# Causal attention: five full half steps on the diagonal, shift rows passed on by GpSimd, maxima matmuls run once

## The chip, the cores and the metric

The kernel runs on one core of one Trainium2 chip. The metric is the device time of one execution in microseconds (us), compared by the median of several runs. The engines are named as in the profile: PE (TensorE matmuls) and PEld (its weight loads), DVE (VectorE), ACT (ScalarE), POOL (GpSimd) and SP (SyncE, which issues the DMAs).

## The reference, cut to what matters

Two transformer layers over 2048 tokens of width 128, with 16 heads of 8. The first has causal attention with rotary positions and a gated feed-forward network; the second has a low-rank attention without a mask and a mixture of eight experts. For the change only the attentions matter:

```python
# first attention
scores = jnp.einsum('bhsd,bhtd->bhst', q, k) / scale
scores = jnp.where(causal[None, None], scores, -jnp.inf)
attn = jax.nn.softmax(scores.astype(jnp.float32), axis=-1).astype(x.dtype)
out = jnp.einsum('bhst,bhtd->bhsd', attn, v)
# second attention: the same without the mask
attn = jnp.einsum('bhqd,bhkd->bhqk', query, key) / scale
attn = jax.nn.softmax(attn, axis=-1)
out = jnp.einsum('bhqk,bhkd->bhqd', attn, value)
```

## The kernel before

The program is a row of phases: norm, projection, attention, output projection, norm, feed-forward, norm, projection, second attention, output projection, norm, gate, experts. Each phase gives every engine its own instruction list, tied together by semaphores. The change is in `attention_phase` alone, which is called for both layers, and in the constant `EXTRA_PASSES`.

**Units.** An attention has 16 units (c, g): a block c of 512 queries (four) and a group g of four heads (four). Unit n needs the maximum over the keys for each of its queries. So the work of a unit is in two parts, made for different units at the same time. *Maxima*: `score_maxima` (PE, L424) computes scores with queries on partitions into a pair of banks, and DVE reduces them (`reduce`, L560). *Steps*: `scores` (L443) computes scores with keys on partitions, ACT takes the exponential (L540) into `k.probs`, and `values` (L456) multiplies with V and sums up in bank 7. The shift by the maxima is folded into extra rows of Q: DVE writes them to `shiftM` (L583, L587), PE turns them (`turn_shift`, L409), and ACT copies them into the rows 32 to 63 and 96 to 127 of Q, for both blocks of heads at once (`take_shift`, L525, two instructions of 32x1024).

**Steps and halves.** A step is one block of 128 keys, for four heads; it has two half steps b of two heads each. In the causal attention a unit has 4(c+1) steps. The last four lie on the diagonal, and `first_col` makes them 512, 384, 256 and 128 columns wide. POOL sets the triangle to zero there (`affine_select`, L509). In the second attention each unit has 16 steps, all full.

**The order on PE** is written out by hand in `unit(n)`: for each half step two score matmuls, then (in the half step where they are due) the queries of unit n+2 (L399, L401) or the turned shift of unit n+1, then the maxima that `plan(n)` gives to this half step, and then a part of the values of the step before. `plan` spreads the last reductions of unit n+1 and the first ones of unit n+2 over the half steps of unit n, in proportion to their widths; the former are urgent, because the shift of unit n+1 needs them. `shift_after` puts the shift two steps before the unit's end.

**Banks.** Scores, queries and the turned shift share three banks in turn (`wait_bank`), so a score matmul waits until ACT is done with what stood in its bank three jobs earlier. Maxima use two pairs of banks in turn: pair m waits for reduction m-2.

**Repetitions.** `score_maxima(m, i, passes)` repeats its pair of matmuls, with the same output, `passes` times: 3 in units with c=0, 2 with c=1, 1 with c=2 and 3 (first attention) and 1 in the units of the second. In the prologue, ahead of unit 0, it is 3 in both attentions.

Of the kernel before, what the change touches and what calls it, by code (L numbers as in the profile page):

```python
# [15 lines left out]
P = 128  # L16
# [5 lines left out]
CW = 512  # L22
# [12 lines left out]
EXTRA_PASSES = (2, 1, 0, 0)  # L35
# [271 lines left out]
def attention_phase(nc, k, layer):  # L307
# [5 lines left out]
    steps = [TC * (c + 1) if causal else T for c, g in units]  # L313
# [9 lines left out]
    first_col = lambda n, kt: max(0, kt - TC * units[n][0]) * P if causal else 0  # L323
# [4 lines left out]
    s_base = [sum(steps[:n]) for n in range(NU + 1)]  # L328

    shift_after = [steps[n] - 2 for n in range(NU)]  # L330

    def exp_bank_jobs():
        for n in (0, 1):
            yield from (("queries", n, b) for b in (0, 1))
        yield ("shift", 0)
        for n in range(NU):
            for kt in range(steps[n]):
                yield from (("scores", n, kt, j) for j in range(HG))
                if kt == 0 and n + 2 < NU:
                    yield from (("queries", n + 2, b) for b in (0, 1))  # L340
                if kt == shift_after[n] and n + 1 < NU:
                    yield ("shift", n + 1)

    e_number = {job: number for number, job in enumerate(exp_bank_jobs())}
    exp_job = lambda n, kt, j: e_number["scores", n, kt, j]

    masks = {n: TC * units[n][0] for n in range(NU)} if causal else {}
    mask_base = lambda n, kt: 2 * (TC * n + kt - masks[n])

    def plan(n):  # L350
        todo = last_reductions(n + 1) + first_reductions(n + 2)
        urgent = len(last_reductions(n + 1))
        widths = [CW - first_col(n, kt) for kt in range(steps[n]) for _ in (0, 1)]
        costs = [len(reductions(m)[i][1]) * (reductions(m)[i][3] + P) for m, i in todo]
        slots, done = [], 0
        for slot in range(len(widths)):
            enough = 0
            while enough < len(todo) and sum(costs[:enough]) * sum(widths) < sum(widths[:slot + 1]) * sum(costs):
# [3 lines left out]
            if slot >= 2 * shift_after[n]:  # L362
                enough = max(enough, urgent)
            if slot == len(widths) - 1:
# [7 lines left out]
    with ExitStack() as ctx:  # L372
        sem = lambda s: ctx.enter_context(nc.semaphore(f"{name}_{s}"))
        e_ready, e_done, pv_done, acc_free = sem("e_ready"), sem("e_done"), sem("pv_done"), sem("acc_free")
        m_ready, m_done, masked = sem("m_ready"), sem("m_done"), sem("masked")
        neg_ready, hi_ready, shift_ready, acc_zero = sem("neg_ready"), sem("hi_ready"), sem("shift_ready"), sem("acc_zero")
# [3 lines left out]
        acc = k.bank[7]  # L380

# [6 lines left out]
        def _(pe):  # L388
# [46 lines left out]
            def scores(n, kt, j):  # L435
                c, g = units[n]
                b, half = divmod(j, 2)
                rows = slice(HALF * half, HALF * half + HALF)
# [713 lines left out]
```

## Time and profile before

| | us |
|---|---|
| median of 3 runs | 1871.16 (1868.39 to 1871.88) |
| the profiled execution | 1862.05 |
| its span, first to last instruction | 1860.1 |

| engine | busy us | share of the span |
|---|---|---|
| PE | 1721.7 | 93% |
| PEld | 812.7 | 44% |
| DVE | 1159.5 | 62% |
| ACT | 1155.4 | 62% |
| POOL | 82.4 | 4% |

All rows of the trace come from the profiled execution, so a sum is made against its 1862.05 us. A line of the profile names the source line, the engine, the operation and the tiles, output first, and its shapes. In a timeline the first two numbers are start and length in us; what stands in brackets is the time for which the engine was idle before it, and what ended that. The granted clock is TensorE's: 1.00 is 2.4 GHz and 0.50 is 1.2 GHz. Matmuls are pipelined, so the distance between the starts of two groups says more of PE's pace than their lengths.

In the trace the first attention has its prologue from 56.5 to 74.0 us, the units with c=0 up to 144.3, c=1 up to 254.9, c=2 up to 396.3 and c=3 up to 561.8 (units 12 and 13 up to 484.8). The prologue of the second attention begins at 825.4 with its first maxima, and its units run from 881.5 to 1566.9.

### The profile page before, as it was taken

To read this page: it belongs to the slowest core of one execution; us is meant where nothing else is said; L and a number is where in the kernel's file an instruction comes from. 1 tells how busy PE (TensorE), PEld (TensorE's weight loads), DVE (VectorE), ACT (ScalarE), POOL (GpSimd) and SP (SyncE) were. 2 spreads that over 40 slices of the span, in tenths; PEclk is the share of its full clock that TensorE was granted. 3 is DMA by queue.
4 is the path that set the end of the run, shared out by engine and by line. 5 is a ranking of instruction groups with operands and counts; after the bars stand their busy time and mean duration, and the time that the engine had idled before them with its cause. 6 is when DMAs were issued, how large, how long until landed. Compare 5 with 4: busy or idle time off the path is not lost. (4 is left out here: it accounts for less than half of the span.)

```text
span 1860.1 us, 32237 instructions
## 1 busy us (share of the span) xinstructions
PE 1721.7 (93%) x13312; PEld 812.7 (44%) x13312; DVE 1159.5 (62%) x1566; ACT 1155.4 (62%) x2092; POOL 82.4 (4%) x158
## 2 busy tenths in 40 slices
PE   6899999999998999678999999999999999599999
PEld 3555444333335444334333333333333334467777
DVE  6576787888505111469899999999999852411111
ACT  3447678678883222231888888888888886143443
POOL 3011101000010000110000000000000000000000
PEclk9799999899998999779999999999999999699999
DMA  3100000000000000100000000000000000000000
GB/s 101 64 1 2 1 2 1 1 1 2 1 1 1 0 0 0 53 1 1 1 1 1 2 1 1 2 1 1 1 2 1 1 1 1 10 26 23 11 23 23
DMA packets 16769, 17.15 MB, mean 9 GB/s; under 512 B 2995, under 2 KB 13696, under 8 KB 16128
## 3 DMA queue, kind: packets, MB, share of 16 engines
q1 hardware_dynamic: 16639, 15.32, 2.6%
q8 instruction: 95, 1.56, 0.3%
q14 instruction: 35, 0.28, 0.1%
HBM read 14.26 MB, written 1.05 MB: 8 GB/s over the span
## 5 line engine op out<-in xcount | busy, mean ns | idle before, releaser
L560 DVE TENSOR_REDUCE maxp<-banks 128x2 f32<-128x1024 f32 (+3 forms) x800 | 945.0, 1201 | 194.1 <-PE banks L424 99.3
L540 ACT ACTIVATE probs<-banks 128x512 f32<-128x512 f32 (+3 forms) x1664 | 854.6, 571 | 222.8 <-PE banks L443 202.9
L456 PE MATMUL banks<-probs,V 128*9 128x256 f32 (+3 forms) x6272 | 491.3, 385 | 6.2 <-POOL probs L509 5.7
L443 PE MATMUL banks<-Q,K 64*128 64x512 f32 (+3 forms) x1664 | 449.8, 487 | 28.0 <-ACT Q L525 20.2
L424 PE MATMUL banks<-K,Q 64*128 64x512 f32 (+3 forms) x2232 | 421.7, 406 | 19.1 <-DVE maxp L560 17.5
L443 PEld LDWEIGHTS banks<-Q,K 64*128 64x128 f32 x1664 | 183.7, 186 | 394.6 <-ACT probs L540 306.8
L424 PEld LDWEIGHTS banks<-K,Q 64*128 64x128 f32 x2232 | 218.7, 194 | 71.9 <-DVE maxp L560 52.9
L456 PEld LDWEIGHTS banks<-probs,V 128*9 128x9 f32 x6272 | 93.2, 88 | 253.3 <-ACT probs L540 187.7
L952 DVE SCALAR_TENSOR_TENSOR x<-banks,wts,x 128x128 f32<-128x128 f32 x128 | 36.0, 345 | 196.6 <-PE banks L915 196.6
L940 ACT ACTIVATE work<-banks,eb 128x512 f32<-128x512 f32 x128 | 86.4, 688 | 104.1 <-PE banks L906 101.7
L915 PEld LDWEIGHTS banks<-work 128*128 128x128 f32 x1024 | 118.1, 192 | 11.5 <-issue 11.5
L906 PE MATMUL banks<-xnT,work 128*128 128x512 f32 x256 | 115.8, 601 | 6.0 <-DMA eb<-in_eb 6.0
L915 PE MATMUL banks<-work 128*128 128x128 f32 x1024 | 118.2, 275 | 0.0
L740 PE MATMUL banks<-work,flex 128*128 128x512 f32 x256 | 110.5, 592 | 0.0
L525 ACT ACTIVATE Q<-banks 32x1024 fp32r<-32x1024 f32 x64 | 65.1, 1017 | 67.7 <-PE banks L409 66.6
L778 DVE TENSOR_TENSOR work<-banks,s_rows 128x128 f32<-128x128 f32 x16 | 3.5, 284 | 122.4 <-PE banks L747 122.4
L591 DVE COPY outT<-banks 128x512 f32<-128x512 f32 x32 | 21.9, 684 | 88.0 <-PE banks L456 87.9
L740 PEld LDWEIGHTS banks<-work,flex 128*128 128x128 f32 x256 | 48.6, 190 | 61.2 <-issue 61.2
L763 ACT ACTIVATE work<-banks,sh 128x512 f32<-128x512 f32 x32 | 22.0, 687 | 82.7 <-PE banks L740 82.7
L509 POOL TENSOR_SCALAR_AFFINE_SELECT probs<-probs 128x256 f32<-128x256 f32 x128 | 52.3, 408 | 468.0 <-ACT probs L540 466.4
L906 PEld LDWEIGHTS banks<-xnT,work 128*128 128x128 f32 x256 | 47.5, 193 | 57.1 <-issue 54.0
L133 PE MATMUL banks<-ident,xn 128*128 128x128 f32 x64 | 17.5, 458 | 26.1 <-DVE xn L115 15.3
(126 smaller groups left out, 836.3 us busy)
## 6 DMA issues: line engine op xcount, KB each, us to landing
tables<-in_tables SPq DMA_DIRECT2D x2, 2048.0 KB, 10.2
work<-in_ew SPq DMA_DIRECT2D x16, 256.0 KB, 2.9
flex<-in_h SPq DMA_DIRECT2D x2, 1024.0 KB, 8.4
x<-in_x SPq DMA_DIRECT2D x4, 256.0 KB, 3.8
out<-x SPq DMA_DIRECT2D x4, 256.0 KB, 2.3
cst<-in_consts SPq DMA_DIRECT2D x1, 865.0 KB, 6.1
flex<-in_w SPq DMA_DIRECT2D x3, 256.0 KB, 2.9
flex<-in_w_qk SPq DMA_DIRECT2D x1, 256.0 KB, 6.1
```

The costliest lines, as they stand in the source:

```text
L424: mm = pe.matmul(out, k.Q[rows, n % 3, b, t * P:(t + 1) * P], k.K[rows, 2 * g + b, a * CW:a * CW + w], start=True, stop=True)
L443: mm = pe.matmul(ebank(e)[:, first:CW], k.K[rows, 2 * g + b, kt * P:(kt + 1) * P], k.Q[rows, n % 3, b, first:CW], start=True, stop=True)
L456: mm = pe.matmul(acc[32 * j:32 * j + HD + 1, low:high], k.V9[:, kt, g * HG + j, :], k.probs[:, slot + j, low:high], start=(kt == 0), stop= ...
L509: pool.affine_select(out=tile, in_=tile, compare_op=ALU.is_ge, fill=0.0, base=0, pattern=[[0, 2], [1, P]], channel_multiplier=-1).then_inc ...
L525: copy = act.activation(k.Q[rows, n % 3, :, :], ebank(e)[rows, :].unsqueeze(1).to_broadcast([HALF - SHIFT_ROW, 2, CW]), ACT.Copy)
L540: act.activation(k.probs[:, HG * (s % 2) + j, first:CW], ebank(e)[:, first:CW], ACT.Exp, scale=scale).then_inc(e_done, 1)
L560: dve.tensor_reduce(dst, src, AX.X, ALU.max).then_inc(m_done, 1)
L740: mm = pe.matmul(hb[m % 2][:, :], w[:, b, m * P:(m + 1) * P], src[:, b, :], start=(b == 0), stop=(b == HB - 1))
L906: pe.matmul(ub[m][:, :], k.ew1[:, q, m * P:(m + 1) * P], k.xnT[:, c * CW:(c + 1) * CW], start=True, stop=True).then_inc(up_ready, 1)
L915: mm = pe.matmul(yb[c % 2][:, t * P:(t + 1) * P], k.hid[:, c % 2, b, t * P:(t + 1) * P], k.ew2[:, q, b, :], start=(b == 0), stop=(b == HB ...
L940: act.activation(k.hid[:, c % 2, m, :], ub[m][:, :], ACT.Gelu, bias=k.eb1[:, q, m:m + 1]).then_inc(act_ready, 1)
L952: dve.scalar_tensor_tensor(k.x[:, i, :], yb[c % 2][:, t * P:(t + 1) * P], k.wts[:, i, bass.ds(e, 1)], k.x[:, i, :], ALU.mult, ALU.add).the ...
```

## The change

The first attention's diagonal has five half steps of full width in place of eight of falling width. The first diagonal step is as before. The `mixed` step puts the second key block (384 columns) and the fourth (128) side by side into one bank for each head. The `narrow` step has one half step: the third key block of 256 columns for two heads in each of two banks. Exponentials are all 512 columns wide and their tiles go round in eights, each with its own release. POOL masks the first column block of each piece: one instruction for the first half and for the narrow step, two for a mixed half. Values of the mixed and narrow steps are multiplied whole.

The shift is turned in the second last half step of a causal unit (before: in the sixth of the eight diagonal ones). In the second attention it stays in half step 29 of 0 to 31. ACT copies the shift rows for block 0 only (two instructions of 32x512), and POOL copies them on to block 1 (two more), in both attentions. PE waits for POOL (`spread_done`) ahead of the second half step of the next unit. `plan` now spreads by the number of half steps and has the urgent maxima ready two half steps ahead of the shift in the first attention.

Every maxima pair runs once, in all units and in both prologues.

```diff
-EXTRA_PASSES = (2, 1, 0, 0)
+EXTRA_PASSES, FIRST_PASSES = (0, 0, 0, 0), 1
...
+    def score_steps(n):
+        c = units[n][0]
+        whole = lambda kt: [[[(j, kt, 0, 0)] for j in (2 * b, 2 * b + 1)] for b in (0, 1)]
+        if not causal:
+            return [whole(kt) for kt in range(T)]
+        first, second, third, fourth = range(TC * c, TC * c + TC)
+        mixed = [[[(j, second, P, 0), (j, fourth, 3 * P, 3 * P)] for j in (2 * b, 2 * b + 1)] for b in (0, 1)]
+        narrow = [[[(half, third, 2 * P, 0), (2 + half, third, 2 * P, 2 * P)] for half in (0, 1)]]
+        return [whole(kt) for kt in range(first + 1)] + [mixed, narrow]
...
-    shift_after = [steps[n] - 2 for n in range(NU)]
+    shift_at = [len(halves[n]) - (2 if causal else 3) for n in range(NU)]
+    urgent_by = [shift_at[n] - (2 if causal else 1) for n in range(NU)]
...
-            while enough < len(todo) and sum(costs[:enough]) * sum(widths) < sum(widths[:slot + 1]) * sum(costs):
+            while enough < len(todo) and sum(costs[:enough]) * number < (slot + 1) * sum(costs):
                 enough += 1
             if slot < 2:
                 enough = min(enough, urgent)
-            if slot >= 2 * shift_after[n]:
+            if slot >= urgent_by[n]:
                 enough = max(enough, urgent)
...
+                if s == 0 and b == 0:
                     pe.wait_ge(e_done, e_number["shift", n] + 1)
+                if s == 0 and b == 1:
+                    pe.wait_ge(spread_done, 2 * n + 2)
+                for piece in range(len(jobs[0])):
+                    for x in (0, 1):
+                        e = e_number["scores", n, s, b, x]
+                        j, kt, low, at = jobs[x][piece]
+                        if piece == 0:
+                            wait_bank(e)
+                        block, half = divmod(j, 2)
+                        rows = slice(HALF * half, HALF * half + HALF)
+                        mm = pe.matmul(ebank(e)[:, at:at + CW - low], k.K[rows, 2 * g + block, kt * P:(kt + 1) * P],
+                                       k.Q[rows, n % 3, block, low:CW], start=True, stop=True)
...
+            def values_part(n, s, b, of):
+                if s == 0 or s == len(step_list[n]) - 1 and causal or of == 1:
+                    if b == of - 1:
+                        values(n, s, "whole")
                 else:
+                    values(n, s, ("first", "second")[b])
...
             for item in first_reductions(0) + last_reductions(0) + first_reductions(1):
-                score_maxima(*item, 1 + EXTRA_PASSES[0])
+                score_maxima(*item, FIRST_PASSES)
...
+        @block.gpsimd
+        def _(pool):
+            def spread_shift(n):
+                pool.wait_ge(e_done, e_number["shift", n] + 1)
+                if n and causal:
+                    pool.wait_ge(masked, masks_done(n - 1, halves[n - 1][shift_at[n - 1]][0]))
+                for half in (0, 1):
+                    pool.tensor_copy(k.Q[shift_rows(half), n % 3, 1, :], k.Q[shift_rows(half), n % 3, 0, :]
+                                     ).then_inc(spread_done, 1)
+                    pool.wait_ge(spread_done, 2 * n + half + 1)
...
+            spread_shift(0)
+            for n in range(NU):
+                for h, (s, b) in enumerate(halves[n]):
+                    if s in diagonal_steps(n):
+                        mask_probs(n, s, b)
+                    if h == shift_at[n] and n + 1 < NU:
+                        spread_shift(n + 1)
...
                 for half in (0, 1):
-                    rows = slice(HALF * half + SHIFT_ROW, HALF * half + HALF)
-                    copy = act.activation(k.Q[rows, n % 3, :, :],
-                                          ebank(e)[rows, :].unsqueeze(1).to_broadcast([HALF - SHIFT_ROW, 2, CW]), ACT.Copy)
+                    copy = act.activation(k.Q[shift_rows(half), n % 3, 0, :], ebank(e)[shift_rows(half), :], ACT.Copy)
                 copy.then_inc(e_done, 1)
```

## Rows read from the trace of the kernel before

**Rows 1.** Windows: length, then busy PE, PEld, DVE, ACT, POOL; granted clock; DMA

```profile
56.50:70.60 14.10, 12.97 (x145) 10.29 (x144) 9.77 (x13) 0.78 (x2) 0.00 (x0) 0.75 0.51 167
74.00:144.30 70.30, 66.47 (x675) 39.53 (x674) 44.62 (x53) 36.88 (x80) 12.94 (x32) 0.93 0.01 2
144.30:254.90 110.60, 104.12 (x1033) 50.28 (x1029) 83.10 (x86) 71.51 (x144) 13.21 (x33) 0.97 0.01 1
254.90:396.30 141.40, 131.83 (x1278) 55.17 (x1274) 118.45 (x118) 105.96 (x208) 13.06 (x32) 0.96 0.00 1
396.30:484.80 88.50, 85.75 (x819) 34.56 (x815) 71.87 (x68) 70.56 (x137) 6.53 (x16) 0.92 0.01 1
484.80:561.80 77.00, 71.89 (x670) 26.88 (x667) 10.76 (x13) 64.13 (x130) 6.54 (x16) 0.96 0.00 1
...
357.00:367.30 10.30, 10.30 (x81) 5.32 (x79) 6.54 (x8) 4.27 (x9) 0.00 (x0) 0.50 0.01 2
...
1142.60:1185.70 43.10, 42.33 (x386) 15.18 (x384) 39.48 (x37) 37.53 (x69) 0.00 (x0) 1.00 0.01 1
```

**Rows 2.** Timeline, second attention, a boundary: start, length, work [idle before]

```profile
1093.79 0.66 PE L409 MATMUL banks<-identr,shiftM 128*128 128x128 f32 x4
...
1094.38 0.50 PE L424 MATMUL banks<-K,Q 64*128 64x512 f32 x2
...
1094.91 2.04 ACT L525 ACTIVATE Q<-banks 32x1024 fp32r<-32x1024 f32 x2
...
1097.01 1.11 PE L443 MATMUL banks<-Q,K 64*128 64x512 f32 x2 [0.37 <-ACT Q L525]
...
1098.39 2.44 DVE L560 TENSOR_REDUCE maxp<-banks 128x2 f32<-128x1024 f32 x2 [1.04 <-PE banks L424]
...
1100.57 0.50 PE L399 MATMUL banks<-qb,sel 32*128 32x512 f32 x1
...
1101.90 0.51 PE L424 MATMUL banks<-K,Q 64*128 64x512 f32 x2
```

**Rows 3.** Groups by form, ACT: busy us, mean ns | idle before

```profile
L540 ACT ACTIVATE probs<-banks 128x512 f32<-128x512 f32 x1472 | 790.7, 596 | 174.5 <-PE banks L443 156.0
...
L525 ACT ACTIVATE Q<-banks 32x1024 fp32r<-32x1024 f32 x64 | 65.1, 1017 | 67.7 <-PE banks L409 66.6
```

**Rows 4.** Timeline, first attention, end of unit 8

```profile
279.20 0.62 PE L456 MATMUL banks<-probs,V 128*9 128x256 f32 x8 [0.23 <-POOL probs L509]
...
283.52 1.23 DVE L560 TENSOR_REDUCE maxp<-banks 128x2 f32<-128x1024 f32 x1 [1.82 <-PE banks L424]
...
285.27 0.62 PE L443 MATMUL banks<-Q,K 64*128 64x128 f32 x2 [0.76 <-ACT Q L525]
```

**Rows 5.** Timeline, prologue of the second attention, a maxima group run three times

```profile
862.40 0.96 PE L424 MATMUL banks<-K,Q 64*128 64x512 f32 x6 [0.20 <-DVE maxp L560]
```

**Rows 6.** Groups by form, POOL

```profile
L271 POOL TENSOR_TENSOR flex<-flex 128x512 f32<-128x512 f32 x16 | 24.4, 1527 | 251.7 <-DVE flex L250 235.8 <-DVE flex L241 15.9
...
L80 POOL CAST sel<-cst 128x1024 fp32r<-128x1024 f32 x1 | 1.1, 1107 | 0.0
...
L79 POOL CAST identr<-cst 128x128 fp32r<-128x128 f32 x1 | 0.3, 332 | 7.5 <-DMA ident<-in_consts 7.5
```

**Rows 7.** Timeline, unit 0 of second attention: half clock to 889.5, then full

```profile
885.44 0.63 PE L443 MATMUL banks<-Q,K 64*128 64x512 f32 x2
...
886.29 1.25 PE L443 MATMUL banks<-Q,K 64*128 64x512 f32 x2
...
887.90 1.80 PE L456 MATMUL banks<-probs,V 128*9 128x512 f32 x8
...
889.63 0.51 PE L443 MATMUL banks<-Q,K 64*128 64x512 f32 x2
...
890.29 0.62 PE L456 MATMUL banks<-probs,V 128*9 128x256 f32 x8
...
890.84 0.52 PE L443 MATMUL banks<-Q,K 64*128 64x512 f32 x2
```

More of the change, by code:

```diff
@@ L312, in attention_phase @@
     NU = len(units)
-    steps = [TC * (c + 1) if causal else T for c, g in units]
     def reductions(n):
@@ L336, in exp_bank_jobs, with masks_done @@
         for n in range(NU):
[L337 to L341, printed above, removed]
+            for h, (s, b) in enumerate(halves[n]):
+                yield from (("scores", n, s, b, x) for x in (0, 1))
+                if h == 1 and n + 2 < NU:
+                    yield from (("queries", n + 2, q) for q in (0, 1))
+                if h == shift_at[n] and n + 1 < NU:
                     yield ("shift", n + 1)
     e_number = {job: number for number, job in enumerate(exp_bank_jobs())}
-    exp_job = lambda n, kt, j: e_number["scores", n, kt, j]
-    masks = {n: TC * units[n][0] for n in range(NU)} if causal else {}
-    mask_base = lambda n, kt: 2 * (TC * n + kt - masks[n])
+    def masks_done(n, s):
+        count = 0
+        for m in range(n + 1):
+            for t in diagonal_steps(m):
+                if (m, t) <= (n, s):
+                    count += sum(1 if [at for _, _, _, at in half[0]] == [0, 2 * P] else len(half[0]) for half in step_list[m][t])
+        return count
     def plan(n):
@@ L454, in values @@
+            def values(n, s, part):
+                g = units[n][1]
+                last = part == "second" or part == "whole"
+                if s in diagonal_steps(n):
+                    pe.wait_ge(masked, masks_done(n, s))
+                else:
+                    pe.wait_ge(e_done, e_number["scores", n, s, 1, 1] + 1)
+                if s == 0:
                     pe.wait_ge(acc_free, n + 1)
-                for j in range(HG):
-                    mm = pe.matmul(acc[32 * j:32 * j + HD + 1, low:high], k.V9[:, kt, g * HG + j, :],
-                                   k.probs[:, slot + j, low:high], start=(kt == 0), stop=(kt == steps[n] - 1 and high == CW))
@@ L458, in values @@
-                if high == CW:
-                    mm.then_inc(pv_done, 1)
-            def values_part(n, kt, b):
-                first = first_col(n, kt)
-                middle = (first + CW) // 2
-                if kt == 0 or CW - first < 2 * P:
-                    if b == 1:
-                        values(n, kt, first, CW)
-                elif b == 0:
-                    values(n, kt, first, middle)
+                todo = sorted(pieces(n, s), key=lambda item: (item[1], item[0]))
+                for j, kt, low, at, tile in todo:
+                    middle = (CW - low) // 2
+                    a, z = {"whole": (0, 2 * middle), "first": (0, middle), "second": (middle, 2 * middle)}[part]
+                    end = s == len(step_list[n]) - 1 and last and kt == todo[-1][1]
+                    mm = pe.matmul(acc[32 * j:32 * j + HD + 1, low + a:low + z], k.V9[:, kt, g * HG + j, :],
+                                   k.probs[:, tile, at + a:at + z], start=(s == 0), stop=end)
@@ L496, in _ @@
             for b in (0, 1):
[L497 to L510 removed]
+                values_part(NU - 1, len(step_list[NU - 1]) - 1, b, 2)
```

125 lines of the change are left out of this document (63 added, 62 removed).

## The prediction

> **What bounds the kernel now.** I read the page's busy shares first: TensorE (PE) is near full, VectorE (DVE) and ScalarE (ACT) under two thirds. Those are averages over unlike stages, so I cut both attentions into stretches [rows 1]. The first attention (74.0 to 561.8) is four stages of four units, one for each query block c; the second (881.5 to 1566.9) is sixteen units of about 43.1 us. In the second, DVE is busy 39.48 of 43.10 us: an off-diagonal half step gives it one maxima reduction (1.22 us), and PE's own half step has nearly the same length, 0.67 (scores and maxima) + 0.55 (values) = 1.22 us, read as the distances between starts in the warm half of [rows 7]. So I looked for where DVE's 3.6 idle us of a unit lie. One hole, 1.04 us, comes just after the shift is turned [rows 2]. It belongs to the shift copy: two ACT instructions of 1.017 us each [rows 3] hold one of the three score banks for 2.04 us, and the score pair at 1097.01 waits until they are done.
>
> In the first attention the units with c of 1 to 3 end in narrow steps. There the reader is to see holes in all three engines: PE waits 0.23 us for a GpSimd mask and 0.76 us for the shift copy, and DVE idles 1.82 us with reductions still to do [rows 4]. After such an end the granted clock can be down: 357.0 to 367.3, just behind the start of unit 11, runs at 0.50 with PE busy all of it [rows 1]. In c=0 and c=1 part of PE's time is repetition: every maxima pair is run three times or twice.
>
> **The change, part by part.**
>
> *Repetitions.* With passes as coded, 14 pairs in the first prologue, 8, 8, 14 and 16 in the four c=0 units are run two times too often, and 16, 16, 20 and 24 in the c=1 units once. In the units that is 92 + 76 = 168 extra pairs; an extra 512-column pair costs (0.96 - 0.50)/2 = 0.23 us of PE, from six matmuls against two [rows 2, 5], so at most 39 us of PE time. In the second attention's prologue 44 reductions lose their repetitions too, but there each group of six ends in a wait for DVE [rows 5]; the cover is DVE's reduction, 1.15 us or more against 0.96, and I cost that removal at nothing. Without that cover it would be worth 44 x 0.46 = 20 us.
>
> *Five half steps for eight.* A unit has 8c+5 half steps instead of 8c+8, and 16c+10 exponentials instead of 16c+16. Columns stay the same, so ACT loses six starts and no columns. A full one takes 790.7/1472 = 0.54 us of ACT [rows 3]; the six starts I set at nothing for c up to 3, since DVE or PE is later there.
>
> *Shift copy.* ACT's two instructions write 512 columns instead of 1024. At 0.54 us for 512 columns [rows 3] 2.04 becomes 1.1 us. GpSimd then makes two 32x512 copies in turn, in both layers. No such copy is in the trace. The nearest rows are its casts, 0.332 us for 128 columns and 1.107 for 1024 [rows 6]; the line through them gives 0.66 us at 512. The upper bound is the two-input 128x512 addition at 1.53 us, the lower the 128-column cast. I take 0.66, so block 1's shift rows are ready some 1.4 us after ACT is done. PE's wait for it stands before the second half step of the next unit. In the second attention that half step would start about 2.9 us after ACT is done, so even two copies of 1.4 us stay hidden. In the first, GpSimd's narrow mask is queued behind the copies, and PE needs it only after the next unit's queries; from starts and durations I get mask ready 4.9, needed 6.5 us after the mixed step's second scores, and the copies themselves ready at 4.3 against 4.6. With 1.5 us copies this turns into 1.3 us a unit over fifteen starts, 20 us.
>
> The Trainium skill, page "GPSIMD Engine Reference", section 4.1, calls one-input work on GpSimd roughly line-rate, and its section 3.1 gives 1.03 cycles an element; as an estimate from that page that is 0.44 us for 512 elements before its start-up. By it the copies would be hidden even better; the casts' row is the dearer one, and no run here has shown the copy itself.
>
> *Sum for c=1 to 3.* PE, a unit, at full clock: 0.34 x (8c+5) for scores (half of the 0.67) + 0.3 for the extra pieces, values 0.55 x 8c + 1.0 (first key block, whole) + 1.1 (mixed, whole) + 0.55 (narrow), queries and shift 1.33 + 0.59, mask matmuls 0.6 (an estimate), and 0.34 a reduction [rows 2, 7]. The reductions done are 70 in c=1, 102 in c=2, 60 in units 12 and 13. That is 81, 120 and 77 us. DVE: its busy time now, 83.10, 118.45 and 71.87 us [rows 1], which the change leaves alone, plus the idle time that stays, 3.6 - 1.04 = 2.5 us a unit: 93, 128.5 and 77. I take the later of the two and 0.5 us a unit for what two engines in turn lose: 95, 130.5 and 78.5 against 110.6, 141.4 and 88.5. Units 14 and 15 have nearly no reductions, and ACT is late there: 116 x 0.54 + 1.1 = 64 us, plus 2 us a unit, 68 against 77.0. So 15.5 + 11 + 10 + 9 = 45.5 us. What is late next is DVE in c=1 and c=2, PE in 12 and 13. The fuller boundary should also spare the clock most of its falls; that is inside these sums, which run at full clock.
>
> *c=0.* Units 0 to 3 take 70.3 us. At full clock they would be 10.5, 10.5, 17 and 18.5 (DVE's 44.62 us and its idle places), 56.5 in all. But in units 2 and 3 six to eight reductions are now bunched in the third half step, where PE does one pair in 1.2 us and waits. The prologue before ran at half clock for half its time even with repetitions (the stretch's mean is 0.75) [rows 1], and the change thins it. Cold, scores plus maxima take 0.85 us for 0.66, and a whole step's values 1.73 us for about 1.0 [rows 7]; the same sum at those steps gives 14 us for units 0 and 1 and 17 for 2 and 3, with waits for DVE 15.5, 15.5, 20.5 and 22, or 73.5. I take 70, no gain, between these ends, plus 3 us for c=1 beginning cold. The first prologue goes from 14.1 to about 11, DVE's 9.77 us [rows 1] being late there: 3 us.
>
> The Trainium skill, page "TensorE: Matmul & The Clock Gate", Part 1, says the array is throttled by default and activity releases it. It speaks against dropping the repetitions; the trace agrees in 357.0 to 367.3 [rows 1], which follows a boundary with waits, and I price it as a rival.
>
> *Second attention.* Fifteen boundaries lose the 1.04 us hole [rows 2], 15.6 us, and the prologue's shift 1 us: 16.6.
>
> Total 45.5 + 0 - 3 + 3 + 16.6 = 62 us. The profiled execution took 1862.05 us (span 1860.1) and becomes 1800; it lies 9 us under the median 1871.16, from which I get **1809**.
>
> **The rivals.**
>
> *Cold through c=0 and c=1.* For it: single passes, bunched reductions. Against: the off-diagonal mix of c=1 is that of the second attention, which runs 43.10 us at clock 1.00 with single passes [rows 1]. Price: the sum at cold steps is 120 us for c=1 instead of 95, and 3.5 more in c=0; less the 3 counted, 26 us. 1835. Chance 0.12.
>
> *Cold through c=2 as well.* This is the one that ends slower. The same sum gives 178 us for c=2 instead of 130.5: 47 more, 1882. It decides once cold units cost more than 62 us, that is from about the third unit of c=2. Against it stands the same row. 0.04.
>
> *GpSimd takes the place of the shift wait.* 1.5 us copies, or masks queued behind them: 20 us, all in the first attention, 1829. For: the mixed step has two masks a half where the old had one, and PE already waits for masks. 0.14.
>
> *The clock never falls after the prologue.* c=0 at 56.5 and no cold start: 17 us better, 1792. 0.08.
>
> *It doesn't do what it says*, the holes being held by the bank order and not by the shift copy: the second attention stays, and half of the diagonal's gain goes, 1809 + 17 + 23 = 1849. Against: the wait at 1097.01 ends with the copy [rows 2]. 0.04.
>
> **How the numbers follow.** The forecast keeps 0.58. Its own range is 1796 to 1822, from the ends of c=0. Taking in the GpSimd bound, the warm case and most of the cold one, the range is 1785 to 1843. A difference under 0.2% (3.7 us) can't be told from none. Faster 0.93, same 0.02, slower 0.05: slower is the second rival and a little for mixtures of it with the third.
>
> **What would show it.** A unit of the second attention at 42.0 us, with no DVE hole after the shift; first attention stages near 70, 95, 130, 78 and 68; the shift copies near 0.55 us and GpSimd's near 0.66; PE never long at a wait for GpSimd. It is wrong if c=1 runs at clock 0.5, if PE stands at the second half step of a unit, or if c=2 stays above 135 us at full clock.

## The result, and the profile after

The changed kernel takes 1792.22 us in the median (1789.71 to 1804.01) against 1869.78 (1865.09 to 1871.88) before. The ratio on record is 0.9606, 95% interval 0.9561 to 0.9652; that of the two medians is 0.9585. The forecast was 1809. Six executions of the changed kernel are on record: four took 1790 to 1794 us at a mean granted clock of 0.933 to 0.938, and two took 1804 us at 0.927. The profiled one is of the latter (1804.01 us, span 1802.3), while the profiled one of the kernel before was quicker than its median. So the two traces differ by 58 us of span where the medians differ by 78.

The windows of the kernel after, cut like [rows 1] where the first exponential of a unit starts, some 0.6 to 1.2 us behind its first score pair (columns as in [rows 1]; the last row is one unit of the second attention):

```profile
70.50:138.10 67.60, 58.59 (x428) 29.68 (x426) 44.46 (x53) 30.54 (x58) 16.89 (x37) 0.65 0.00 1
138.10:230.90 92.80, 85.83 (x816) 37.03 (x814) 80.92 (x86) 64.56 (x120) 16.75 (x36) 0.98 0.01 2
230.90:359.90 129.00, 123.00 (x1212) 51.36 (x1210) 119.02 (x119) 99.34 (x184) 16.23 (x36) 1.00 0.01 1
359.90:438.30 78.40, 77.92 (x786) 31.28 (x784) 72.00 (x68) 66.93 (x125) 8.48 (x19) 1.00 0.01 1
438.30:512.00 73.70, 70.91 (x638) 26.23 (x636) 10.79 (x14) 62.40 (x118) 7.84 (x17) 0.95 0.01 1
1001.80:1044.20 42.40, 42.12 (x386) 15.18 (x384) 39.53 (x37) 36.73 (x69) 1.22 (x2) 1.00 0.01 2
```

Set against [rows 1], with the working's forecast for each stretch:

| stretch | before | after | change | forecast |
|---|---|---|---|---|
| up to unit 0 | 74.0 | 70.5 | -3.5 | -3 |
| c=0 | 70.3 | 67.6 | -2.7 | 0 |
| c=1 | 110.6 | 92.8 | -17.8 | -12.5 |
| c=2 | 141.4 | 129.0 | -12.4 | -11 |
| units 12, 13 | 88.5 | 78.4 | -10.1 | -10 |
| units 14, 15 | 77.0 | 73.7 | -3.3 | -9 |
| up to the second attention's unit 0 | 319.7 | 318.1 | -1.6 | -1 |
| second attention | 685.7 | 677.7 | -8.0 | -15.6 |
| rest | 293.0 | 294.5 | +1.5 | 0 |

In c=1 the forecast is the stage's 15.5 less the 3 us counted for a cold start. DVE's busy time in c=2 is as before, 119.02 for 118.45 us; the stretch is shorter because DVE stands idle less. In c=0 the clock is 0.65, where it was 0.93. In the stretch up to the second attention's unit 0 it is 0.82 for 0.89: with single passes it stays at 0.50 from 760.5 to 839.0, through that prologue, and the stretch is 1.6 us shorter all the same.

A boundary of the second attention, to be read beside [rows 2]:

```profile
1039.29 0.66 PE L437 MATMUL banks<-identr,shiftM 128*128 128x128 f32 x4
...
1040.50 1.19 ACT L579 ACTIVATE Q<-banks 32x512 fp32r<-32x512 f32 x2
...
1041.83 1.28 POOL L542 CAST Q<-Q 32x512 fp32r<-32x512 f32 x2 [41.09 <-ACT Q L579]
...
1042.07 0.79 PE L478 MATMUL banks<-Q,K 64*128 64x512 f32 x2
...
1043.13 2.44 DVE L612 TENSOR_REDUCE maxp<-banks 128x2 f32<-128x1024 f32 x2 [0.27 <-PE banks L452]
...
1043.58 0.51 PE L478 MATMUL banks<-Q,K 64*128 64x512 f32 x2
```

The shift copies take 1.19 us for 2.04, PE's next pair has no wait for them, and DVE's hole before its next reductions is 0.27 us for 1.04. The pair at 1043.58 is the next unit's first. GpSimd's two copies end at 1043.11, and the second half step of the next unit, which needs them, begins at 1044.79.

The end of unit 8 in the first attention, beside [rows 4]:

```profile
255.78 0.62 PE L497 MATMUL banks<-probs,V 128*9 128x256 f32 x8 [0.19 <-POOL probs L556]
...
256.76 0.66 PE L437 MATMUL banks<-identr,shiftM 128*128 128x128 f32 x4
...
257.89 2.45 DVE L612 TENSOR_REDUCE maxp<-banks 128x2 f32<-128x1024 f32 x2 [1.04 <-PE banks L452]
...
258.03 1.19 ACT L579 ACTIVATE Q<-banks 32x512 fp32r<-32x512 f32 x2
...
259.00 1.05 PE L497 MATMUL banks<-probs,V 128*9 128x384 f32 x16
...
259.28 1.28 POOL L542 CAST Q<-Q 32x512 fp32r<-32x512 f32 x2 [0.44 <-ACT Q L579]
...
259.98 0.50 PE L478 MATMUL banks<-Q,K 64*128 64x512 f32 x2
...
261.22 0.51 PE L478 MATMUL banks<-Q,K 64*128 64x512 f32 x2
```

PE waits 0.19 us for a mask and not at all for the shift; the next unit's two first half steps begin at 259.98 and 261.22. DVE's hole is 1.04 us for 1.82. GpSimd's copies end at 260.56, before the second half step.

The groups by form behind the new durations:

```profile
L593 ACT ACTIVATE probs<-banks 128x512 f32<-128x512 f32 x1568 | 843.1, 596 | 203.9 <-PE banks L478 157.0
...
L579 ACT ACTIVATE Q<-banks 32x512 fp32r<-32x512 f32 x64 | 37.7, 589 | 66.2 <-PE banks L437 65.1
...
L542 POOL CAST Q<-Q 32x512 fp32r<-32x512 f32 x64 | 39.0, 610 | 725.2 <-ACT Q L579 723.2
...
L556 POOL TENSOR_SCALAR_AFFINE_SELECT probs<-probs 128x512 f32<-128x512 f32 x16 | 10.2, 637 | 11.5 <-ACT probs L593 10.8
```

### The profile page after: what moved, and what is told of

Read it like the earlier page. It is cut to its first block and busy times, and to the rows that moved or that the text cites. A ratio compares the mean times of both kernels' runs of the same rounds, so it can differ in the third digit from the quotient of the medians.

```text
span 1802.3 us, 31760 instructions
## 1 busy us (share of the span) xinstructions
PE 1667.7 (93%) x12488; PEld 768.9 (43%) x12488; DVE 1157.5 (64%) x1566; ACT 1115.9 (62%) x1996; POOL 116.3 (6%) x206
## 5 line engine op out<-in xcount | busy, mean ns | idle before, releaser
L612 DVE TENSOR_REDUCE maxp<-banks 128x2 f32<-128x1024 f32 (+3 forms) x800 | 942.9, 1200 | 137.1 <-PE banks L452 71.1
L593 ACT ACTIVATE probs<-banks 128x512 f32<-128x512 f32 x1568 | 843.1, 596 | 203.9 <-PE banks L478 157.0
L478 PE MATMUL banks<-Q,K 64*128 64x512 f32 (+3 forms) x1664 | 435.0, 484 | 8.4 <-ACT probs L593 5.0
L452 PE MATMUL banks<-K,Q 64*128 64x512 f32 (+3 forms) x1664 | 375.8, 434 | 35.0 <-DVE maxp L612 34.4
L478 PEld LDWEIGHTS banks<-Q,K 64*128 64x128 f32 x1664 | 180.0, 188 | 363.9 <-ACT probs L593 287.0
L452 PEld LDWEIGHTS banks<-K,Q 64*128 64x128 f32 x1664 | 177.7, 198 | 85.6 <-DVE maxp L612 70.3
L542 POOL CAST Q<-Q 32x512 fp32r<-32x512 f32 x64 | 39.0, 610 | 725.2 <-ACT Q L579 723.2
L579 ACT ACTIVATE Q<-banks 32x512 fp32r<-32x512 f32 x64 | 37.7, 589 | 66.2 <-PE banks L437 65.1
L556 POOL TENSOR_SCALAR_AFFINE_SELECT probs<-probs 128x256 f32<-128x256 f32 (+1 forms) x112 | 47.9, 441 | 365.0 <-ACT probs L593 364.3
```

The source lines that it names most:

```text
L452: mm = pe.matmul(out, k.Q[rows, n % 3, b, t * P:(t + 1) * P], k.K[rows, 2 * g + b, a * CW:a * CW + w], start=True, stop=True)
L478: mm = pe.matmul(ebank(e)[:, at:at + CW - low], k.K[rows, 2 * g + block, kt * P:(kt + 1) * P], k.Q[rows, n % 3, block, low:CW], start=True ...
L542: pool.tensor_copy(k.Q[shift_rows(half), n % 3, 1, :], k.Q[shift_rows(half), n % 3, 0, :]).then_inc(spread_done, 1)
L556: pool.affine_select(out=part, in_=part, compare_op=ALU.is_ge, fill=0.0, base=0, pattern=[[0, part.shape[1]], [1, P]], channel_multiplier= ...
L579: copy = act.activation(k.Q[shift_rows(half), n % 3, 0, :], ebank(e)[shift_rows(half), :], ACT.Copy)
L593: act.activation(k.probs[:, number % 8, :], ebank(e), ACT.Exp, scale=scale).then_inc(e_done, 1)
```

## The experiments

All are timed in the same manner, beside runs of the kernel before on the same chip (medians 1870.5 to 1873.3), and a ratio is to those. Lengths of stretches are read from each run's own windows, cut in the same way.

### The repetitions put back

```diff
-EXTRA_PASSES, FIRST_PASSES = (0, 0, 0, 0), 1
+EXTRA_PASSES, FIRST_PASSES = (2, 1, 0, 0), 3
```

> The changed kernel with the repetitions of before put back (three times in c=0 and in both prologues, twice in c=1). Theory 1 (repetitions were PE time on the path, worth at most 168 x 0.23 = 39 us, most of it covered by DVE, and the clock in c=0 eats its share): c=1 grows from 92.8 to about 103 us, c=0 stays near 67 us because full clock and repetitions cancel, total about 10 us more than the changed kernel's 1792, so 1802. Theory 2 (the half clock of c=0 costs more than the repetitions did): the granted clock of c=0 returns to above 0.9 and the kernel is faster than the changed one, 1785 or less. Theory 3 (the repetitions were the larger part of the gain): 1820 or more.

Measured: 1805.93 us median (1799.31 to 1807.19), ratio to before 0.9658 (0.9621 to 0.9695). Windows of c=0 and c=1:

```profile
70.20:133.10 62.90, 56.83 (x606) 34.51 (x604) 44.77 (x53) 30.31 (x56) 16.76 (x36) 1.00 0.01 2
133.10:233.50 100.40, 97.37 (x968) 46.91 (x964) 82.80 (x86) 64.79 (x121) 16.76 (x36) 1.00 0.01 2
```

c=1 takes 100.4 us for 92.8, and c=0 62.9 for 67.6 with its clock back at 1.00. So in these two traces dropping the repetitions gives 7.6 us in c=1 and takes 4.7 in c=0, 3 us net. The medians of the whole kernel are 14 us apart, or 11 when each is set against the kernel before beside it, and the two ratios' intervals overlap. The profiled executions don't show that gap: this one took 1799.31 us, the quickest of its kernel, and the changed kernel's was at its slow end. By the medians theory 1 holds; where in the untraced executions the rest of its 11 to 14 us lies is not shown. About c=0 theory 1 was too mild in this trace.

### Single passes in the kernel before

```diff
-EXTRA_PASSES = (2, 1, 0, 0)
+EXTRA_PASSES = (0, 0, 0, 0)
```

> The kernel before with one pass for every maxima pair, nothing else changed. Theory 1: c=1 falls from 110.6 to about 99 us, c=0 stays within 4 us of 70.3 with a granted clock under 0.8, the prologue gains 3 us; total about 1857. Theory 2 (the half clock costs more than the repetitions): c=0 above 75 us or c=1 below clock 0.85, total 1870 or more. Theory 3: 1845 or less.

Measured: 1875.80 us median (1865.33 to 1884.03), ratio 1.0022 (0.9994 to 1.0051). Windows of c=0, c=1 and c=2:

```profile
72.00:136.10 64.10, 56.90 (x497) 27.27 (x493) 44.19 (x53) 36.75 (x80) 13.01 (x32) 0.78 0.00 1
136.10:250.10 114.00, 106.06 (x882) 45.69 (x882) 82.42 (x86) 71.98 (x145) 13.00 (x32) 0.79 0.00 1
250.10:400.50 150.40, 140.97 (x1275) 59.47 (x1273) 119.37 (x118) 106.50 (x209) 13.00 (x32) 0.89 0.01 1
```

Theory 1 fell, and theory 2 holds in c=1: its clock is 0.79 and it takes 114.0 us, more than the 110.6 with repetitions. Even c=2, whose own passes were single before too, goes from clock 0.96 to 0.89 and from 141.4 to 150.4 us. Alone, this part of the change is worth nothing or less: the median lies 3 us above that of the kernel before beside it, and the interval takes in 1.

### GpSimd's copies in the kernel before

```diff
-                    copy = act.activation(k.Q[rows, n % 3, :, :],
-                                          ebank(e)[rows, :].unsqueeze(1).to_broadcast([HALF - SHIFT_ROW, 2, CW]), ACT.Copy)
+                    copy = act.activation(k.Q[shift_rows(half), n % 3, 0, :], ebank(e)[shift_rows(half), :], ACT.Copy)
...
+                    for half in (0, 1):
+                        pool.tensor_copy(k.Q[shift_rows(half), n % 3, 1, :], k.Q[shift_rows(half), n % 3, 0, :]
+                                         ).then_inc(spread_done, 1)
...
+                if kt == 0 and j == 2:
+                    pe.wait_ge(spread_done, 2 * n + 2)
```

> The kernel before with the shift rows copied by ScalarE for block 0 only and passed on to block 1 by GpSimd, with the old eight half steps and the old repetitions. Theory 1 (the shift copy's time in a score bank is what makes the hole at a unit's start): units of the second attention fall from 43.1 to 42.4 us (15 x 0.7 = 10 us), and the first attention loses most of its 0.76 us wait in fifteen boundaries (about 8 us); total about 1852. Rival (GpSimd's copies, two of 0.61 us in turn, take the place of the wait in the first attention): PE waits there for GpSimd by 0.5 us or more a unit, the first attention doesn't gain, total 1860.

Measured: 1828.23 us median (1825.03 to 1830.95), ratio 0.9774 (0.9734 to 0.9815): 44 us under the kernel before beside it, over twice what was expected. The traces' spans differ by 34 us. Windows of c=1, c=2 and units 12 and 13:

```profile
137.70:242.80 105.10, 101.39 (x1033) 48.86 (x1030) 82.94 (x86) 67.69 (x145) 17.28 (x40) 1.00 0.01 1
242.80:379.50 136.70, 129.98 (x1276) 54.29 (x1275) 118.37 (x118) 102.55 (x209) 17.56 (x41) 0.98 0.01 1
379.50:461.00 81.50, 80.28 (x819) 32.14 (x815) 71.75 (x68) 68.40 (x136) 8.80 (x21) 1.00 0.01 2
```

Units 17 to 29 of the second attention take 549.7 us together for 560.8, the 11 us that were expected. In the first attention c=1 loses 5.5 us, c=2 4.7 and units 12 and 13 7.0, and their clock is 1.00, 0.98 and 1.00 where it was 0.97, 0.96 and 0.92. PE's waits for ScalarE's shift copy between 74 and 560 us (total, times, longest), in the kernel before, here, and in "The diagonal alone" below:

```profile
PE banks L443 <- ACT Q L525: 9.9, 13, 1.2
...
PE banks L446 <- ACT Q L539: 1.0, 3, 0.3
...
PE banks L476 <- ACT Q L574: 1.2, 6, 0.3
```

So 8.9 us of waiting went, at most 1.2 at a boundary, and units 12 and 13 lost 3.5 us each. The rest goes with the half clock that came after such boundaries before and is nearly gone in this trace.

### ScalarE copies both blocks in the changed kernel

```diff
-                    copy = act.activation(k.Q[shift_rows(half), n % 3, 0, :], ebank(e)[shift_rows(half), :], ACT.Copy)
+                    copy = act.activation(k.Q[shift_rows(half), n % 3, :, :],
+                                          ebank(e)[shift_rows(half), :].unsqueeze(1).to_broadcast([HALF - SHIFT_ROW, 2, CW]), ACT.Copy)
...
-                if s == 0 and b == 1:
-                    pe.wait_ge(spread_done, 2 * n + 2)
```

> The changed kernel with ScalarE copying the shift rows for both blocks, as before, and no GpSimd copies. Theory 1: the second attention's units return from 42.4 to 43.1 us (10 us), and in the first attention the 2.04 us copy now has one half step less behind it, so a wait of about 1 us a unit comes back (15 us); total about 1792 + 25 = 1817. Rival (in the first attention GpSimd's copies stand in for ScalarE's at equal price, as PE also waits 0.22 us for them): only the second attention loses, total about 1802.

Measured: 1819.42 us median (1813.70 to 1820.76), ratio 0.9718 (0.9676 to 0.9759), 27 us above the changed kernel, near theory 1's 25. The place is not all as it had it. Units 17 to 29 take 562.2 us for 551.0. In the first attention c=1 is equal (93.1), c=2 takes 131.2 for 129.0 and units 12 and 13 82.0 for 78.4, with a clock of 0.96: about 6 us, not 15, in this execution.

### The diagonal alone

Two edits of the changed kernel together, and with them PE's wait for GpSimd and GpSimd's copies are left out, as in the experiment before:

```diff
-EXTRA_PASSES, FIRST_PASSES = (0, 0, 0, 0), 1
+EXTRA_PASSES, FIRST_PASSES = (2, 1, 0, 0), 3
...
-                    copy = act.activation(k.Q[shift_rows(half), n % 3, 0, :], ebank(e)[shift_rows(half), :], ACT.Copy)
+                    copy = act.activation(k.Q[shift_rows(half), n % 3, :, :],
+                                          ebank(e)[shift_rows(half), :].unsqueeze(1).to_broadcast([HALF - SHIFT_ROW, 2, CW]), ACT.Copy)
```

> The five half steps alone: the changed kernel with the repetitions of before and with ScalarE copying the shift rows for both blocks. Theory 1 (parts add up): the changed kernel without repetitions removed stands at 1806 and without GpSimd's copies at 1819, so 1806 + 27 = 1833; against before that is 38 us for the diagonal. Theory 2 (the diagonal's gain and the copies' gain are the same hole at the unit's end, counted twice): with only one of them most of both is there, as GpSimd's copies alone already gave 44 us; then the diagonal alone gives 1825 or less. Theory 3 (it is mostly the clock, and either edit is enough to keep it up): units 12 and 13 at a granted clock of 0.98 or more and under 83 us together.

Measured: 1833.33 us median (1830.41 to 1834.97), ratio 0.9794 (0.9753 to 0.9834). Windows of c=1, c=2 and units 12 and 13:

```profile
140.20:240.50 100.30, 97.26 (x968) 46.83 (x964) 82.77 (x86) 68.22 (x120) 11.66 (x28) 1.00 0.01 2
240.50:371.50 131.00, 124.33 (x1213) 52.16 (x1209) 118.83 (x119) 102.30 (x184) 11.64 (x28) 1.00 0.01 1
371.50:450.90 79.40, 78.54 (x787) 31.73 (x785) 72.00 (x68) 68.46 (x126) 5.99 (x14) 1.00 0.01 1
```

The total is theory 1's 1833, but that sum already holds the overlap. Each set against the kernel before beside it, the copies alone give 44 us, the diagonal alone 37, and both together 67 ("The repetitions put back"), so some 15 us are common to both. Part of what is common is the wait itself, as theory 2 says, though its total of 1825 was not reached: PE's waits for the shift copy fall from 9.9 us to 1.0 with the copies and to 1.2 with the diagonal. The clock is another part, as theory 3 says: units 12 and 13 are at 1.00 with either edit, 81.5 and 79.4 us. That either edit is enough to keep the clock is not shown. The experiment before runs the same code in these two units (their passes were single all along), and its trace has 0.96 and 82.0 us.

### Both with single passes: the last corner

The kernel before with GpSimd's copies, still in eight half steps, and in it:

```diff
-EXTRA_PASSES = (2, 1, 0, 0)
+EXTRA_PASSES = (0, 0, 0, 0)
```

> The kernel before with GpSimd's copies and with single passes, and the old eight half steps: the last corner of the three edits. Theory 1 (single passes pay once the boundaries are short enough to keep the clock, whichever edit shortens them): c=1 near 96 us at clock 0.95 or more, total 1828 - 14 = 1814. Rival (with the narrow half steps left in, single passes cost the clock again, as they did with nothing else changed): c=1 or c=2 at clock 0.90 or less, total 1825 or more.

Measured: 1824.51 us median (1820.99 to 1830.21), ratio 0.9747 (0.9690 to 0.9803). Windows of c=0, c=1 and c=2:

```profile
70.70:139.10 68.40, 63.49 (x494) 31.32 (x491) 44.49 (x53) 33.51 (x81) 17.76 (x41) 0.65 0.00 1
139.10:245.20 106.10, 100.03 (x880) 42.85 (x878) 82.16 (x86) 68.35 (x144) 17.01 (x39) 0.85 0.01 1
245.20:381.50 136.30, 128.82 (x1276) 53.45 (x1274) 118.35 (x118) 102.53 (x208) 17.63 (x41) 0.99 0.01 1
```

c=1 is at clock 0.85 and takes 106.1 us, against 105.1 with its repetitions. The rival holds for the clock, and its total of 1825 is missed by half a microsecond; theory 1's 1814 is out. Now all eight corners are measured (medians, us; the two at the left top and right bottom are the kernels before and after). The last row sets each median against the kernel before beside it, as those differ by up to 3 us:

| | eight half steps, ACT copies | eight, GpSimd copies | five, ACT copies | five, GpSimd copies |
|---|---|---|---|---|
| repetitions | 1869.8 | 1828.2 | 1833.3 | 1805.9 |
| single passes | 1875.8 | 1824.5 | 1819.4 | 1792.2 |
| removing them | +6 | -4 | -14 | -14 |
| the same, each against its own before | +3 | -3 | -16 | -11 |

The removal of the repetitions pays only where the diagonal is full; in the eight half steps neither difference is clear of the spread of the executions. With the full diagonal, which engine copies makes no difference to it that these medians can show. What it is in the new diagonal that makes the difference is not separated: with the full half steps came a later shift and another `plan` of the maxima, and no run has one without the others.

### Where c=0 loses its clock

```diff
-EXTRA_PASSES, FIRST_PASSES = (0, 0, 0, 0), 1
+EXTRA_PASSES, FIRST_PASSES = (0, 0, 0, 0), 3
```

> The changed kernel with three passes in the two prologues alone. Theory 1 (c=0's own density decides its clock, through the bunch of reductions in its third half step): c=0 begins at full clock but falls within units 1 to 3; its mean stays under 0.85 and it takes 65 to 68 us; total 1788 to 1794. Rival (c=0 is cold because it begins cold): c=0 at clock 0.95 or more and 60 us or less, total 1782.

Measured: 1801.89 us median (1794.34 to 1803.60), ratio 0.9614 (0.9568 to 0.9660). Window of c=0:

```profile
72.40:138.50 66.10, 56.90 (x424) 29.68 (x424) 44.52 (x53) 30.54 (x57) 16.91 (x37) 0.68 0.00 1
```

Repetitions in the prologues alone don't hold c=0's clock, 0.68 and 66.1 us, within theory 1's figures. But c=0 didn't begin at full clock as theory 1 has it: the clock is at 0.50 from 71.4 to 85.1, then 1.00 up to 105.6, and again 0.50 from 105.6 to 115.8 and from 119.2 on. So the later falls come after full clock, in units 2 and 3, and speak for c=0's own work; a start at full clock was not tested. The total is 8 us above theory 1's upper bound.

```diff
-EXTRA_PASSES, FIRST_PASSES = (0, 0, 0, 0), 1
+EXTRA_PASSES, FIRST_PASSES = (2, 0, 0, 0), 3
```

> The changed kernel with three passes again in the c=0 units and both prologues, single passes in c=1. Theory 1 (only c=0 needs the activity): c=0 at 63 us and clock near 1.00 as with all repetitions back, c=1 at 92.5 us and clock 1.00; total 1792 - 5 = 1787. Rival (c=1 falls to half clock as the kernel before did with single passes): c=1 above 100 us, 1795 or more.

Measured: 1799.71 us median (1793.42 to 1801.57), ratio 0.9606 (0.9561 to 0.9650). Windows of c=0 and c=1:

```profile
72.20:135.10 62.90, 56.81 (x610) 34.41 (x608) 44.75 (x53) 30.34 (x57) 16.78 (x37) 1.00 0.01 2
135.10:228.90 93.80, 87.92 (x818) 37.73 (x816) 81.07 (x86) 64.46 (x121) 16.74 (x36) 0.95 0.01 1
```

c=0 gets its 62.9 us and clock 1.00, as expected, but the total isn't below the changed kernel's. The profiled execution has 1.7 us more up to unit 0 and 1 us each more in c=1, c=2 and units 12 and 13. That leaves it 5.6 us of span ahead of the changed kernel's profiled execution, while the medians say 7.5 us behind. The ratios on record are the same, 0.9606 for both, so neither is shown to be the faster.

Nor is c=0's time a matter of the repetitions alone. In the trace of "The diagonal alone", which has them, c=0 begins at 0.50 and takes 68.9 us at a mean of 0.89; in that of the first kernel under "More work for VectorE", which has single passes there, it takes 62.5 us at 0.71. One trace a kernel doesn't settle what full clock in c=0 is worth.

### GpSimd's copies made twice

```diff
-                    pe.wait_ge(spread_done, 2 * n + 2)
+                    pe.wait_ge(spread_done, 4 * n + 4)
...
-                for half in (0, 1):
+                for i, half in enumerate((0, 1, 0, 1)):
...
-                    pool.wait_ge(spread_done, 2 * n + half + 1)
+                    pool.wait_ge(spread_done, 4 * n + i + 1)
```

> The changed kernel with GpSimd making its two copies of the shift rows twice over, 2.6 us in place of 1.3. Theory 1 (in the second attention the copies have 1.6 us of slack, in the first PE already waits 0.2 us for them): units 17 to 29 stay at 42.4 us, the first attention's boundaries grow by about 1.2 us each, 18 us in all, total 1810. Rival (the bank order, not the copies, holds PE at a unit's start): the first attention grows by under 5 us, total under 1797. Third: the second attention grows as well, 1825 or more.

Measured: 1817.65 us median (1810.11 to 1825.17), ratio 0.9707 (0.9653 to 0.9760), 25 us above the changed kernel. The waits for the copies in total, and one of them at the second half step of a unit (in the changed kernel the same two sums are 1.7 and 0.2 us):

```profile
PEld banks L478 <- POOL Q L542: 19.9, 26, 2.2
...
PE banks L478 <- POOL Q L542: 10.2, 11, 1.6
...
369.67 0.50 PE L478 MATMUL banks<-Q,K 64*128 64x512 f32 x2 [1.03 <-POOL Q L542]
```

Units 17 to 29 stay at 551.1 us for 551.0: the slack there is real. The first attention pays, 2.8 us in c=1, 7.3 in c=2, 5.6 in units 12 and 13 and 3.4 in 14 and 15, with the clock down to 0.95, 0.95, 0.94 and 0.93. Theory 1 has the place right. These four stages make 19 us, close to its 18; the medians have 25, and the spans of the two traces 14. The clock falls where waits were put in, the reverse of "GpSimd's copies in the kernel before".

### More work for VectorE where the queries are built

```diff
-            while enough < len(todo) and sum(costs[:enough]) * number < (slot + 1) * sum(costs):
+            early = 1 if slot and not causal else 0
+            while enough < len(todo) and sum(costs[:enough]) * number < min(slot + 1 + early, number) * sum(costs):
...
                     scores(n, s, b)
+                    now = slots[h]
                     if h == 1 and n + 2 < NU:
+                        if now and not causal:
+                            score_maxima(*now[0], 1 + EXTRA_PASSES[units[n][0]] if causal else 1)
+                            now = now[1:]
                         build_queries(n + 2)
```

So `plan` runs one half step ahead from the second half step on, in the second attention.

> The changed kernel, in the second attention: the half step that builds queries gets two maxima pairs, one ahead of the queries and one behind, and the last half step gets none. Theory 1 (a unit there is 40.3 us of VectorE and 40.6 of TensorE, and the rest is the 1.65 us in which VectorE has nothing while TensorE builds queries): units 17 to 29 fall from 42.4 to about 41.2 us, 16 us in all, total 1776. Rival (the hole moves behind the queries or to the unit's end): 42.0 us or more, total 1786 or more.

Measured: 1790.80 us median (1787.66 to 1795.29), ratio 0.9576 (0.9538 to 0.9613). The same in both attentions, for the units with c of 1 to 3 (the condition `not causal` becomes `not causal or units[n][0]`):

> The same in the first attention too, for the units with c of 1 to 3. Theory 1: c=1, c=2 and units 12 and 13 lose another 0.5 to 1 us a unit, 7 us in all against the other kernel of this pair, since VectorE bounds units 6, 7, 10 and 11 there. Rival (the cap on the urgent maxima in the first two half steps keeps the extra pair away, or TensorE is late there): no difference from the other, within 3 us.

Measured: 1801.35 us median (1799.21 to 1802.72), ratio 0.9622 (0.9587 to 0.9658). VectorE's timeline at a boundary of the second attention, the former kernel:

```profile
903.28 2.44 DVE L617 TENSOR_REDUCE maxp<-banks 128x2 f32<-128x1024 f32 x2 [0.86 <-PE banks L453]
...
906.96 2.46 DVE L617 TENSOR_REDUCE maxp<-banks 128x2 f32<-128x1024 f32 x2 [1.24 <-PE banks L453]
...
909.85 1.22 DVE L617 TENSOR_REDUCE maxp<-banks 128x2 f32<-128x1024 f32 x1 [0.43 <-PE banks L453]
```

The hole at the queries, 1.65 us in the changed kernel, has shrunk to 0.43 us, and one of 1.24 has come at the unit's end, where the last half step has no pair now. Units 17 to 29 take 548.0 us for 551.0: the rival's case, and no difference from the changed kernel that the medians can show. In the first attention the same edit costs: the median is 10.6 us above the former kernel's, which neither its theory (7 us less) nor its rival (within 3 us) had. c=1 takes 95.7 us there, units 12 and 13 82.6, with a clock of 0.96 in both. No version clearly beats the changed kernel.

## Why the prediction was right, point by point

**The sums for c=1 to 3 held.** The later of PE's sum and DVE's busy time with its idle places, and 0.5 us a unit, gave 95, 130.5 and 78.5 us; measured are 92.8, 129.0 and 78.4, at clock 0.98 to 1.00. DVE was busy 80.92 us in c=1 for the 83.10 assumed, and idle for 3.0, 2.5 and 3.2 us a unit where 2.5 was told. The mask order on GpSimd went as told: GpSimd's copies held PE at one matmul, for 0.2 us, and at three weight loads in the whole changed kernel.

**The attribution inside them was incomplete.** The step said of the clock's falls that their sparing "is inside these sums", and gave it no price of its own. GpSimd's copies alone, by the same reasoning 18 us, gave 44 by the medians. What the clock's part of that is can be estimated from the kernel before: 33 of its executions beside the experiments run from 1859.3 us at a mean clock of 0.951 to 1879.7 at 0.937, about 14 us for every 0.01. GpSimd's copies lift the middle of the mean clocks from 0.9415 to 0.9565, which at that rate is some 21 of the 44 us. The corners show that the edits don't add: the copies and the diagonal share some 15 us, in which the shift wait itself is counted twice.

**Repetitions.** The upper bound of 39 us of PE time was safe, and so was "most of it covered". By the medians they are worth 11 to 16 us behind a full diagonal, and within 3 us of nothing without it. The Trainium skill, page "TensorE: Matmul & The Clock Gate", Part 1, calls the throttled state the default, which activity releases, and so spoke against dropping them. The traces agree in the kernel before, for c=1 (114.0 us at 0.79 without them, 110.6 at 0.97 with them). For c=0 two of three traces with them and the new diagonal agree (62.9 us at 1.00, against 67.6 at 0.65), and the third (68.9 at 0.89) doesn't. The rival "cold through c=0 and c=1" is partly what the kernel before does with single passes, at 0.78 and 0.79. In the changed one it did not come: c=1 keeps 0.98, and with eight half steps in place of the new diagonal 0.85.

**c=0.** Taken as 70, between 56.5 at full clock and 73.5 at half; it came to 67.6 at 0.65. No trace has it under 62.5 us, not even two at clock 1.00 (62.9, with the repetitions), so the lower end of 56.5 was set too low.

**The shift copy.** ScalarE's pair takes 1.19 us for the 1.1 assumed: the two, of 0.589 us each, don't overlap as exponentials in a row do. GpSimd's copy takes 0.610 us for the 0.66 from the line through the casts. The copies are hidden in the second attention, as the doubled ones show; in the first they are nearly so.

**Second attention: the term that was mis-sized.** I let the whole hole of 1.04 us go and counted 15.6 us. It went to 0.27, so units 17 to 29 take 42.4 us each, not 42.0. That is 0.7 us a unit. What is late next seems to be the bank: of the pair at 1042.07 the second matmul starts only at 1042.37, just after an exponential of ScalarE that ends at 1042.32. That is read from the trace, and no run tested it. And in the profiled execution units 30 and 31 came out 1.4 and 1.1 us longer than before. PE waited in unit 30 for the shift rows of the last unit, whose maxima are only just ahead of it, and half clock followed:

```profile
1463.75 1.08 PE L437 MATMUL banks<-identr,shiftM 128*128 128x128 f32 x4 [1.69 <-DVE shiftM L639]
...
1464.88 1.19 ACT L579 ACTIVATE Q<-banks 32x512 fp32r<-32x512 f32 x2 [1.64 <-PE banks L437]
...
1465.74 0.79 PE L478 MATMUL banks<-Q,K 64*128 64x512 f32 x2
```

The granted clock is 0.50 from 1463.6 to 1470.4. The mechanism was right, and the size half of what was told: 8 us in the trace, of which units 17 to 29 make 9.8 and the last two take 2.5 back.

**Units 14 and 15.** Told 68 us, measured 73.7. ScalarE is late there, as told, with 62.40 us busy; the 2 us a unit for its gaps was too little:

```profile
454.07 2.08 ACT L593 ACTIVATE probs<-banks 128x512 f32<-128x512 f32 x4 [0.21 <-PE banks L478]
...
454.47 0.75 PE L478 MATMUL banks<-Q,K 64*128 64x512 f32 x2
...
455.21 0.62 PE L497 MATMUL banks<-probs,V 128*9 128x256 f32 x8
...
456.35 1.09 ACT L593 ACTIVATE probs<-banks 128x512 f32<-128x512 f32 x2 [0.20 <-PE banks L478]
```

Even in a full half step ScalarE waits about 0.2 us at such places; that PE's pair is late there because its bank is not free is my reading and was not tested. A fall of the clock came in unit 15, 0.50 from 477.2 to 484.0 (0.95 for the two). With the clock at 1.00 the same code takes 71.1 us in the kernel with its repetitions back, with ScalarE busy 62.19. So the gaps are about 4.5 us a unit for the 2 told, and the clock's fall is the other 2.6 us.

**The total** of the terms was 62 us, and the traces give 58. That the medians give 78 is not in my working. The executions of the changed kernel span 1790 to 1804 us with granted clocks from 0.938 to 0.927, and the traced one lies at the slow end, while that of before lies 9 us under its median. The step from the trace to the median added those 9 us and took nothing for such a place of the changed kernel's trace. So the median was inside the wide range in part for a reason that I hadn't priced: the mean clock, and the time with it, differs from one execution to the next. It is below the forecast's own range of 1796 to 1822 and falls on the 1792 of the rival "the clock never falls after the prologue", whose mechanism did not come (c=0 at 0.65 and 67.6 us); that is chance. The own range was also not what the ends of c=0 give, which is 1795.5 to 1812.5.

## What to carry to other kernels

Where TensorE is bounded by a neighbour and close to losing its clock, price a stall by the half clock that can follow it too and not by its own length alone; here an edit expected to save 18 us of waiting gave 44 by the medians, about half of it with the clock. Repeated matmuls that keep the clock up could go here once the diagonal was full, and were worth nothing to remove before: try such parts in all combinations, since each one alone gave another sign or size. Before a single trace decides a matter of a few microseconds, look where its execution lies among the others. And sum each stage by the later of two engines; that was good to 2.2 us in each of the three stages where the clock stayed up and both engines were priced.

## What the runs showed of the hardware that I had not expected

The granted clock drops after boundaries in which TensorE is busy most of the time. In the kernel before, 0.50 from 357.0 to 367.3 [rows 1] follows these two waits of PE, the only ones that its timeline shows from 347 to 357 us:

```profile
350.04 0.51 PE L456 MATMUL banks<-probs,V 128*9 128x192 f32 x8 [0.34 <-POOL probs L509]
...
353.68 0.62 PE L443 MATMUL banks<-Q,K 64*128 64x128 f32 x2 [0.75 <-ACT Q L525]
```

In the trace with shorter waits, units 12 and 13 have 1.00 for 0.92. In the traced execution of the kernel before with single passes, c=2, whose own instructions are the same, has 0.89 for 0.96. Equal code can differ by as much: units 12 and 13 of the new diagonal with ScalarE's copies had 1.00 and 79.4 us in one trace, 0.96 and 82.0 in another. GpSimd's cast of 32x512 takes 0.610 us, and its mask over 512 elements 0.637 where one over 256 takes 0.41.
